# Graph product of the last stage in two row halves, router of the last stage laid out twice

## The chip, the cores and the metric

One program on one core of a Trainium2 chip. The metric is the device time of the whole program in microseconds (us), from the first to the last instruction with what the launch adds. Times of single instructions are read from one profiled execution.

## The reference, cut to what matters

The kernel computes two rounds of (graph layer, then mixture of experts) over 128 graphs of 64 nodes with 128 channels. The change touches only the second round:

```python
# adj: (128, 64, 64), regrouped; x: tokens x 128 channels
d = (sum(adj, -1) + 1e-5) ** -0.5
x = x + (d * adj * d) @ (layernorm(x) @ W) + b            # graph layer: a 64 x 64 matrix per graph
f = layernorm(x)
r = relu(f @ router_w1 + router_b1)                       # 128 -> 64
p = softmax(r @ router_w2 + router_b2); top-2 of 6 experts # 64 -> 6
x = x + sum over the two chosen experts of weight * mlp_e(f)   # 128 -> 128 -> 128 -> 128
```

A graph has 64 nodes, so two graphs fill the 128 rows (partitions) of a tile, and the product with `adj` mixes only rows of the same graph.

## The kernel before, in words

The program has three stages. The first (0 to 346 us of the profile) is the first round up to its router. The second ("blocks", 354 to 652 us) runs 136 blocks of 128 gathered rows through their expert, one block after the other. The third ("the sweep", from 653 us to the end) is the second round: 16 groups `g` of 512 tokens, each as `TG` = 4 tiles of 128 tokens (two graphs each).

In the sweep every engine runs its own list of steps for an iteration, and the lists of one iteration hold steps of several groups: PE (TensorE) works on `g[0]`, `g[1]` and `g[2]` at once. No scheduler is involved. The order on each engine is the order of the calls in its `body`, and semaphores tie the engines together. The steps of PE that matter, in their order: `aT` (graph product, L2175), `c(1)`, `gnn` (times the weight, L2186), `c(2)`, `gateT_`, then a long row of expert products, `f3T` (transposition of the normalised rows), `b(2)`, `b(3)`, `rh` (router layer 1, L2203), `b(4)`, `a(4)`, `logits` (router layer 2, L2212), `a(2)`, `b(5)`, `c(0)`, `a(1)`, `a(0)`, and the next `aT`. `a`, `b` and `c` are the three layers of the experts (L2245, L2269, L2277).

What waits for what around them:
- `aT` writes PSUM bank 2; ACT (ScalarE) copies it to `tT` (L1569), and only then can PE do `gnn`. Between them PE has `c(1)`.
- `logits` writes bank 7; DVE (VectorE) adds the bias (`lg_`, L1897), finds the largest (`top_`, L1905), does the gating product `m(2)` (L1892, tiles prod<-act,gate_bc), then `dtop_` (L1933) and `xn_`. ACT waits for `dtop` with `etop_` (L1591), and its next step is `ra(2)` (L1555), the evacuation of `a(2)`. PE's `a(0)` uses the bank of `a(2)` and waits for `ra(2)`.
- POOL (GpSimd) issues eight gathers in an iteration (L1481), and between them the elementwise `rs` (L1499) and `xb_` (L1491, 128x512, both operands in SBUF). The fifth gather stands just ahead of `xb_`.

The first group's graph product does not run in the sweep. `first_group` places it, one tile for each block, into the last blocks (L2114, L2116), in PSUM bank 0.

A float32 product is seen in the profile as two LDWEIGHTS and two MATMUL records, which I call its two pieces; `aT` and `logits` have four products and so eight pieces in each group. `PEld` is the loading of the stationary operand.

In `aT` the moving operand is `adjt[p][:, t, :]`, a 128 x 128 matrix with one graph in its upper left and one in its lower right quarter; the two other quarters are set to zero by POOL once (L1439), ahead of the load. `rhT` has 64 rows: `logits` uses the upper half of the array alone.

Of the kernel before, what the change touches and what calls it, by code (L numbers as in the profile page):

```python
# [20 lines left out]
P = 128  # L21
# [74 lines left out]
def build(nc, x, adj_t, gnn0_w, gnn0_b, ln1, ln2, wqkv, wo, router0, w13, w2, gnn1_w, gnn1_b,  # L96
# [14 lines left out]
    with ExitStack() as whole:  # L111
# [1089 lines left out]
        with ExitStack() as ctx:  # L1201
# [13 lines left out]
            gw, gb = sb("gw1", [P, C]), sb("gb1", [P, C])  # L1215
            rw1, rw1_hi, rw1_lo = sb("rw1", [P, RH]), sb("rw1_hi", [P, RH], f32r), sb("rw1_lo", [P, RH], f32r)
            rb1, rw2, rb2 = sb("rb1", [RH, 1]), sb("rw2", [RH, 8]), sb("rb2", [P, 8])
            ew1_hi, ew1_lo = sb("ew1_hi", [P, NE1 * C], f32r), sb("ew1_lo", [P, NE1 * C], f32r)
# [4 lines left out]

            adjt = [sb(f"adjt_c{i}", [P, TG, C]) for i in range(2)]
            rows = [sb(f"expert_rows{i}", [P, 2 * TG, C]) for i in range(2)]
# [17 lines left out]
            tabled, TABLE = sem("tabled"), 20  # L1243
            tile_aT, tile_tT, tile_gnn = sem("tile_aT"), sem("tile_tT"), sem("tile_gnn")
# [3 lines left out]
            rhT = sb("rhT", [RH, GT])  # L1248
            lg, top, topi = sb("lg_c", [P, TG, 8]), sb("top_c", [P, TG, 8]), sb("topi_c", [P, TG, 8], u32)
# [13 lines left out]
            gates_stored, stored = sem("gates_stored"), sem("stored")  # L1263
            NW = 14

            B_AT, B_GNN, B_F3T, B_RH, B_LOGITS, B_GATET = 2, 6, 5, 2, 7, 0
            B_A, B_B = (5, 7, 5, 3, 4, 7), (5, 0, 1, 6, 0, 3)
# [79 lines left out]
            with nc.Block() as block:  # L1347
                @block.sync
                def _(sp):
# [30 lines left out]
                    def lda(g, p):  # L1380
                        if g is not None:
                            if first(g):
                                sp.wait_ge(zeroed, 2)
                            if has(g - 2):
                                sp.wait_ge(at["aT"], g - 1)
                            src = adj_t[bass.ds(g * GT, GT), :].rearrange("(t b m) n -> b m t n", b=2, m=NN)
                            for k in range(2):
                                sp.dma_start(adjt[p][k * NN:(k + 1) * NN, :, k * NN:(k + 1) * NN], src[k]).then_inc(ld_adj[p], 16)

# [40 lines left out]
                def _(pool):  # L1430
                    def last_group():

                        G.memset(prod[:, :, HIDP:KC * P], 0.0).then_inc(padded, 1)
                        for n in range(2 * TG):
                            G.indirect_dma_start(
                                out=slots_in, out_offset=bass.IndirectOffsetOnAxis(ap=slot_now0[1][:, n:n + 1], axis=0),
                                in_=flat[1][:, n // 2, :], in_offset=None, bounds_check=ROWS - 1).then_inc(scattered[1], 16)
                            if n in (1, 3):
                                G.memset(adjt[n // 2][:, :, :], 0.0).then_inc(zeroed, 1)  # L1439
                            elif n == 5:  # L1440
                                G.memset(gate[:, :, :], 0.0).then_inc(zeroed, 1)

                    def weights():

                        G.memset(mhalf[:, :], -0.5).then_inc(padded, 1)
                        G.memset(rb2[:, :], -1e30).then_inc(zeroed, 1)
                        G.memset(eb3[:, :], 0.0).then_inc(zeroed, 1)
                        pool.wait_ge(padded, 2)
                        pool.wait_ge(zeroed, 5)
                        for dst, src in ((gw[:, :], gnn1_w), (gb[:, :], gnn1_b.partition_broadcast(P)), (rw1[:, :], r1_w1),  # L1450
                                         (rb1[:, :], r1_b1), (rw2[:, :], r1_w2), (rb2[:, 0:NE1], r1_b2.partition_broadcast(P)),
                                         (ew1[:, :], e_w1), (ew2[:, :], e_w2), (ew3[:, :], e_w3), (eb1[:, :], e_b1), (eb2[:, :], e_b2),
                                         (eb3[0:NE1, :], e_b3), (eb3[8:8 + NE1, :], e_b3), (eb3[16:16 + NE1, :], e_b3)):
# [73 lines left out]
                def _(act):  # L1527
# [36 lines left out]
                    def tT_(g):  # L1564
                        if g is not None:
                            act.wait_ge(at["aT"], g + 1)
                            if has(g - 1):
                                act.wait_ge(at["gnn"], g)
                            S.activation(tT[:, :, :], banks[B_AT][:, :], ACT.Copy).then_inc(at["tT"], 1)  # L1569

# [7 lines left out]
                    def rhr(g):  # L1578

                        if g is not None:  # L1580
                            act.wait_ge(at["rh"], g + 1)
                            if has(g - 1):
                                act.wait_ge(at["logits"], g)
                            S.activation(rhT[:, :], banks[B_RH][0:RH, :], ACT.Relu, bias=rb1[:, :]).then_inc(at["rhr"], 1)

# [58 lines left out]
                def _(dve):  # L1644
# [249 lines left out]
                    def lg_(g):  # L1894
                        if g is not None:
                            dve.wait_ge(at["logits"], g + 1)
                            V.tensor_tensor(lg[:, :, :], banks[B_LOGITS][:, 0:TG * 8].rearrange("p (t e) -> p t e", t=TG),  # L1897
                                            rb2[:, :].unsqueeze(1).broadcast_to([P, TG, 8]), ALU.add).then_inc(router.sem, 1)

# [197 lines left out]
                def _(pe):  # L2097
# [5 lines left out]
                    def first_group(t):  # L2103

                        if t == 0:
                            pe.wait_ge(prepared, 8)
                            pe.wait_ge(ld_adj[0], 32)
                            pe.wait_ge(at["xn"], 1)
# [58 lines left out]
                    def aT(g, p):  # L2167

                        if g is not None:
                            pe.wait_ge(ld_adj[p], pair(g, p) * 2)  # L2170
# [210 lines left out]
```

## Time and profile before

| | |
|---|---|
| time, median of 3 runs | 992.95 us (992.92 to 993.37) |
| span of the profiled execution | 991.6 us |
| PE busy | 930.0 us, 94% of the span |
| DVE / ACT / POOL busy | 73% / 58% / 46% |
| an iteration of the sweep | 20.2 to 21.2 us (start of `logits` to start of the next) |

The profile gives for each stretch what an engine did, and what ended the idle time ahead of an instruction. The profiled execution's span is 1.35 us shorter than the median of the runs, which holds what lies around the span as well. A MATMUL record starts when the instruction is taken up and can include waiting for its weights; so a distance between the starts of two neighbours says more than the length of one.

### The profile page before, as it was taken

Reading aid. Unit: us, or ns where it says so; the run is one execution under the profiler, and the core shown is the slowest. Engines: PE = TensorE matmul, PEld = TensorE weight load, DVE = VectorE, ACT = ScalarE, POOL = GpSimd, SP = SyncE. Lnnn points to the kernel's source line nnn. Section 1 sums busy time; section 2 is a strip of 40 time slices with the busy share of each in tenths; the row PEclk is TensorE's granted clock in tenths of the full one; section 3 lists DMA queues with packets and bytes.
Section 4 is the critical chain, followed back from the end, with each engine's and each line's share of the span. In section 5 each row is a group of like instructions: output and inputs, shape, how many; then the busy total and the mean of one; then the engine's idle time right before and its main releaser. Section 6 shows DMA issues by size and latency. Waiting matters only on the chain.

```text
span 991.6 us, 26476 instructions
## 1 busy us (share of the span) xinstructions
PE 930.0 (94%) x6766; PEld 735.8 (74%) x6767; DVE 721.4 (73%) x3070; ACT 573.6 (58%) x1498; POOL 459.7 (46%) x458
## 2 busy tenths in 40 slices
PE   5899999999999589999999999989999999999998
PEld 4777877787778479999999999965665556555564
DVE  4688888888887556455555546678888888888863
ACT  2587677767777434555555555445455554555554
POOL 2357777777777585002001000256665656656410
PEclk9999999999999889999999999999999999999999
DMA  5411111111110042222222222224333443334422
GB/s 180 134 36 47 44 53 48 43 45 50 48 45 26 35 137 61 64 61 73 67 66 70 62 60 71 68 61 152 112 107 105 137 146 113 106 104 126 149 81 85
DMA packets 88607, 81.32 MB, mean 82 GB/s; under 512 B 26894, under 2 KB 81568, under 8 KB 86256
## 3 DMA queue, kind: packets, MB, share of 16 engines
q1 hardware_dynamic: 78624, 62.21, 20.1%
q0 software_dynamic: 8784, 18.16, 5.8%
q10 hardware_dynamic: 1152, 0.39, 0.2%
q8 instruction: 20, 0.33, 0.1%
q14 instruction: 27, 0.22, 0.1%
HBM read 57.46 MB, written 23.27 MB: 81 GB/s over the span
## 4 chain that ended last, share of the span: by engine, by line
PE 54%; issue 5%; POOL 3%; DVE 2%; ACT 1%; DMA 1%; POOLq 0%; DVEq 0%; ACTq 0%
PE bank L2147 13%; PE bank L2130 10%; PE bank L2277 6%; PE bank L2269 6%; PE bank L2245 5%; PE bank L2155 4%; POOL expert_rows L1481 2%; PE bank L2139 2%; PE bank L2186 1%; PE bank L2212 1%; PE bank L2175 1%; PE bank L2203 1%; ACT h L1555 1%; PE bank L2195 1%; PE bank L2291 1%
## 5 line engine op out<-in xcount | busy, mean ns | idle before, releaser
L1481 POOL DMA_INDIRECT expert_rows<-slots_out,slot_c x128 | 139.5, 1090 | 106.1 <-DVE ys L1728 75.3
L1720 DVE TENSOR_TENSOR prod<-bank,act 128x342 f32<-128x342 f32 x136 | 70.0, 515 | 102.8 <-ACT act L1538 102.6
L362 POOL DMA_INDIRECT slots_in<-flat,slot_now x120 | 120.5, 1004 | 37.7 <-issue 37.5
L2130 PE MATMUL bank<-w_sb,prodT 128*128 x816 | 118.9, 282 | 0.9 <-ACT prodT L1543 0.7
L1538 ACT ACTIVATE act<-bank 128x342 f32<-128x342 f32 x136 | 62.0, 456 | 96.0 <-PE bank L2147 96.0
L2130 PEld LDWEIGHTS bank<-w_sb,prodT 128*128 128x128 f32 x816 | 101.7, 191 | 8.5 <-issue 6.0
L2147 PE MATMUL bank<-w_hi,xT_hi 128*128 x272 | 99.0, 364 | 0.1
L2269 PE MATMUL bank<-h,ew 128*128 128x512 f32 x192 | 97.6, 606 | 0.0
L2147 PE MATMUL bank<-w_hi,xT_lo 128*128 x272 | 87.0, 320 | 0.0
L2147 PE MATMUL bank<-w_lo,xT_hi 128*128 x272 | 86.6, 319 | 0.0
L1555 ACT ACTIVATE h<-bank,eb 128x512 f32<-128x512 f32 x96 | 63.6, 680 | 14.1 <-PE bank L2245 13.8
L1499 POOL TENSOR_TENSOR rs_c<-var_c,mhalf 128x4 f32<-128x4 f32 x16 | 20.2, 1261 | 109.4 <-DVE var_c L1816 109.4
L2245 PE MATMUL bank<-f_hi,ew_hi 128*128 128x512 f32 x96 | 66.3, 691 | 3.9 <-ACT h L1555 3.9
L1548 ACT ACTIVATE xT_hi<-bank 128x128 fp32r<-128x128 f32 x136 | 37.7, 277 | 52.3 <-PE bank L2139 52.3
L2155 PE MATMUL bank<-cst,prod 128*128 128x128 f32 x408 | 66.8, 273 | 0.1
L1543 ACT ACTIVATE prodT<-bank 128x384 f32<-128x384 f32 x136 | 66.1, 486 | 0.9 <-PE bank L2155 0.8
L452 ACT ACTIVATE pr<-sc,nmx 128x64 f32<-128x64 f32 x256 | 62.7, 337 | 1.3 <-DVE nmx L680 1.3
L1562 ACT ACTIVATE flat<-bank,eb 128x512 f32<-128x512 f32 x64 | 43.5, 681 | 26.7 <-DVE ys L1892 17.4
L1506 POOL TENSOR_TENSOR rs_d<-var_d,mhalf 128x4 f32<-128x4 f32 x16 | 17.2, 1076 | 84.3 <-DVE var_d L1864 84.3
L2155 PEld LDWEIGHTS bank<-cst,prod 128*128 128x128 f32 x408 | 52.7, 140 | 3.0 <-DVE prod L1720 0.5
L2147 PEld LDWEIGHTS bank<-w_hi,xT_hi 128*128 128x128 f32 x272 | 51.4, 189 | 2.0 <-issue 1.2
L2147 PEld LDWEIGHTS bank<-w_lo,xT_hi 128*128 128x128 f32 x272 | 52.0, 191 | 0.0
(320 smaller groups left out, 2481.6 us busy)
## 6 DMA issues: line engine op xcount, KB each, us to landing
gate_bc<-gates_dram SPq DMA_DIRECT2D x16, 1536.0 KB
xs<-slots_in SPq DMA_DIRECT2D x136, 64.0 KB, 1.8
slots_out<-ys SPq DMA_DIRECT2D x68, 128.0 KB, 1.8
base_all<-in_x SPq DMA_DIRECT2D x16, 256.0 KB, 2.8
out<-ob SPq DMA_DIRECT2D x16, 256.0 KB, 2.7
w_lo<-in_w SPq DMA_DIRECT2D x1, 2736.0 KB, 9.9
adjt<-in_adj_t SPq DMA_DIRECT2D x32, 64.0 KB, 2.3
slots_in<-flat,slot_now POOLq DMA_INDIRECT x128
```

What stands on the lines that cost most here:

```text
L362: G.indirect_dma_start(out=slots_in, out_offset=bass.IndirectOffsetOnAxis(ap=slot_now0[p][:, n:n + 1], axis=0), in_=flat[p][:, n // 2, :], ...
L452: last = S.activation(pr[:, t, h, :], sc[:, t, h, :], ACT.Exp, scale=SCALE, bias=nmx[:, t * NH + h:t * NH + h + 1])
L1481: G.indirect_dma_start(out=rows[p][:, n, :], out_offset=None, in_=slots_out[0:filled(g) * P, :], in_offset=bass.IndirectOffsetOnAxis(ap=sl ...
L1538: S.activation(act1[:, u % 2, :], banks[1 + u % 2][:, 0:HIDP], ACT.Silu).then_inc(silu_done, 1)
L1543: S.activation(prodT[:, (u - 3) % 2, :], banks[5 + (u - 3) % 2][:, 0:KC * P], ACT.Copy).then_inc(prodT_copied, 1)
L1555: S.activation(h1[n % 3][:, :], banks[B_A[n]][:, :], ACT.Relu, bias=eb1[:, n:n + 1]).then_inc(per["ra"].sem, 1)
L1720: V.tensor_tensor(prod[:, u % 2, 0:HIDP], banks[3 + u % 2][:, 0:HIDP], act1[:, u % 2, :], ALU.mult).then_inc(prod_done, 1)
L2130: last = T.matmul(banks[7][:, 0:C], prodT[:, u % 2, n * P:(n + 1) * P], w2_sb[:, bass.ds(e * (KC * C) + n * C, C)], start=n == 0, stop=n = ...
L2147: last = T.matmul(banks[1 + 2 * n + par][:, 0:HIDP], xx[:, par, :], ww[:, bass.ds(e * (2 * HIDP) + n * HIDP, HIDP)], start=q == 0, stop=q ...
L2155: last = T.transpose(banks[5 + u % 2][:, n * P:(n + 1) * P], prod[:, u % 2, n * P:(n + 1) * P], ident)
L2245: last = T.matmul(banks[B_A[n]][:, :], ww[:, w], ff[p][:, :], start=q == 0, stop=q == 2)
L2269: T.matmul(banks[B_B[n]][:, :], ew2[:, n * C:(n + 1) * C], h1[n % 3][:, :], start=True, stop=True).then_inc(per["b"].sem, 1)
```

## The change

1. `adjt` holds only the 64 columns that are not zero. It is loaded by one DMA for a group instead of two, and is no longer cleared by POOL.
2. `aT` does for each tile two products: rows 0 to 63 (first graph) into bank 2, rows 64 to 127 (second graph) into bank 0, with 64 columns each. ACT copies the two banks to `tT` with two instructions of 128x4x64 instead of one of 128x512.
3. `first_group` does the same with both halves in bank 0, with a wait for the first half ahead of the second.
4. `router_w1`, its bias and `router_w2` are loaded twice, so that `rh` gives each of the 64 outputs twice, in rows 0 to 63 and 64 to 127. `logits` takes the upper rows for tiles 0 and 2 (bank 7) and the lower ones for tiles 1 and 3 (bank 2). DVE adds the bias in two instructions.
5. `aT` waits for `lg` of the group before (it waited for `rhr`) and for `rb4` of the one before that.

```diff
-                            src = adj_t[bass.ds(g * GT, GT), :].rearrange("(t b m) n -> b m t n", b=2, m=NN)
-                            for k in range(2):
-                                sp.dma_start(adjt[p][k * NN:(k + 1) * NN, :, k * NN:(k + 1) * NN], src[k]).then_inc(ld_adj[p], 16)
+                            sp.dma_start(adjt[p][:, :, :], adj_t[bass.ds(g * GT, GT), :].rearrange("(t p) n -> p t n", p=P)).then_inc(ld_adj[p], 16)
...
-                            if n in (1, 3):
-                                G.memset(adjt[n // 2][:, :, :], 0.0).then_inc(zeroed, 1)
...
-                            S.activation(tT[:, :, :], banks[B_AT][:, :], ACT.Copy).then_inc(at["tT"], 1)
+                            for b in range(2):
+                                last = S.activation(tT[:, :, b * NN:(b + 1) * NN], banks[B_AT[b]][:, 0:TG * NN].rearrange("p (t n) -> p t n", t=TG), ACT.Copy)
+                            last.then_inc(at["tT"], 1)
...
-                            V.tensor_tensor(lg[:, :, :], banks[B_LOGITS][:, 0:TG * 8].rearrange("p (t e) -> p t e", t=TG),
-                                            rb2[:, :].unsqueeze(1).broadcast_to([P, TG, 8]), ALU.add).then_inc(router.sem, 1)
+                            for j in range(2):
+                                last = V.tensor_tensor(lg[:, j:TG:2, :], banks[B_LOGITS[j]][:, 0:TG * 4].rearrange("p (t e) -> p t e", t=TG // 2),
+                                                       rb2[:, :].unsqueeze(1).broadcast_to([P, TG // 2, 8]), ALU.add)
+                            last.then_inc(router.sem, 1)
...
-                            T.matmul(banks[0][:, P:2 * P], xn[:, t, :], adjt[0][:, t, :], start=True, stop=True).then_inc(tile_aT if t < TG - 1 else at["aT"], 1)
+                            T.matmul(banks[0][:, P:P + NN], xn[0:NN, t, :], adjt[0][0:NN, t, :], start=True, stop=True).then_inc(tile_half, 1)
+                            pe.wait_ge(tile_half, t + 1)
+                            T.matmul(banks[0][:, P + NN:2 * P], xn[NN:P, t, :], adjt[0][NN:P, t, :], start=True, stop=True).then_inc(tile_aT if t < TG - 1 else at["aT"], 1)
...
                             if exists(g - 1):
-                                pe.wait_ge(at["rhr"], g)
-                            for t in range(TG):
-                                last = T.matmul(banks[B_AT][:, t * P:(t + 1) * P], xn[:, t, :], adjt[p][:, t, :], start=True, stop=True)
+                                pe.wait_ge(router.sem, router.at("lg", g - 1))
+                            if exists(g - 2):
+                                pe.wait_ge(per["rb"].sem, per["rb"].at("rb4", g - 2))
+                            for t in range(TG):
+                                for b in range(2):
+                                    last = T.matmul(banks[B_AT[b]][:, t * NN:(t + 1) * NN], xn[b * NN:(b + 1) * NN, t, :],
+                                                    adjt[p][b * NN:(b + 1) * NN, t, :], start=True, stop=True)
...
-                                last = T.matmul(banks[B_RH][0:RH, :], ww[:, :], ff[p][:, :], start=q == 0, stop=q == 2)
+                                last = T.matmul(banks[B_RH][:, :], ww[:, :], ff[p][:, :], start=q == 0, stop=q == 2)
...
-                                last = T.matmul(banks[B_LOGITS][:, t * 8:t * 8 + 8], rhT[:, t * P:(t + 1) * P], rw2[:, :], start=True, stop=True)
+                                half = slice(t % 2 * RH, (t % 2 + 1) * RH)
+                                last = T.matmul(banks[B_LOGITS[t % 2]][:, t // 2 * 8:t // 2 * 8 + 8], rhT[half, t * P:(t + 1) * P], rw2[half, :], start=True, stop=True)
```

On PE, in an iteration of the sweep, from the last product of `a(0)` to `c(2)`, before (the shape is that of the output):

```order
L2245 MATMUL bank<-f_hi,ew_lo 128x512
L2175 MATMUL bank<-adjt_c,xn_c 128x128 x4
L2277 MATMUL bank<-ys,ew 128x512
L2186 MATMUL bank<-gw,tT_c 128x128 x4
L2277 MATMUL bank<-prod,ew 128x512
```

and in the changed kernel:

```order
L2250 MATMUL bank<-f_hi,ew_lo 128x512
L2178 MATMUL bank<-adjt_c,xn_c 128x64 x8
L2282 MATMUL bank<-ys,ew 128x512
L2190 MATMUL bank<-gw,tT_c 128x128 x4
L2282 MATMUL bank<-prod,ew 128x512
```

The place of every step is the same; four products of 128 columns have become eight of 64. On PE in the last blocks, at the first group's first tile, as a difference:

```order
 L2130 ISA
 L2130 MATMUL bank<-w_sb,prodT 128x128
-L2114 MATMUL bank<-adjt_c,xn_c 128x128
+L2112 MATMUL bank<-adjt_c,xn_c 128x64
+L2114 MATMUL bank<-adjt_c,xn_c 128x64
 L2139 MATMUL bank<-cst,xs 128x128
```

Here too only the product is split, between the same neighbours; L2112 and L2114 are the two halves with the wait between them. On no other engine does a step change its place.

## Rows read from the trace of the kernel before

**Rows 1.** The page, part 1: busy us (share of the span) xinstructions of each engine.

```profile
PE 930.0 (94%) x6766; PEld 735.8 (74%) x6767; DVE 721.4 (73%) x3070; ACT 573.6 (58%) x1498; POOL 459.7 (46%) x458
```

**Rows 2.** Timeline of PE, 711.5 to 725.2: start, us, engine, line, what, [idle before].

```profile
715.39 0.40 PE L2245 MATMUL bank<-f_hi,ew_lo 128*128 128x512 f32 x1
715.72 1.05 PE L2212 MATMUL bank<-rw,rhT 64*128 64x8 f32 x8
716.71 0.51 PE L2245 MATMUL bank<-f_hi,ew_hi 128*128 128x512 f32 x1
717.05 0.40 PE L2245 MATMUL bank<-f_lo,ew_hi 128*128 128x512 f32 x1
...
720.26 0.50 PE L2245 MATMUL bank<-f_hi,ew_hi 128*128 128x512 f32 x1 [0.17 <-ACT h L1555]
...
720.83 0.39 PE L2245 MATMUL bank<-f_hi,ew_lo 128*128 128x512 f32 x1
721.05 1.05 PE L2175 MATMUL bank<-adjt_c,xn_c 128*128 128x128 f32 x8
721.95 1.02 PE L2277 MATMUL bank<-ys,ew 128*128 128x512 f32 x2
722.81 1.15 PE L2186 MATMUL bank<-gw,tT_c 128*128 128x128 f32 x8
```

**Rows 3.** Timeline of PE, 943.5 to 949.8, the same steps twelve groups later.

```profile
943.65 1.05 PE L2212 MATMUL bank<-rw,rhT 64*128 64x8 f32 x8
...
948.56 1.05 PE L2175 MATMUL bank<-adjt_c,xn_c 128*128 128x128 f32 x8
```

**Rows 4.** Timeline of PE's weight loads, 715.3 to 724.2.

```profile
722.79 0.97 PEld L2186 LDWEIGHTS bank<-gw,tT_c 128*128 128x128 f32 x8 [0.65 <-ACT tT_c L1569]
```

**Rows 5.** Timeline of DVE, 716.7 to 720.4.

```profile
716.82 0.19 DVE L1897 TENSOR_TENSOR lg_c<-bank,rb 128x32 f32<-128x32 f32 x1 [0.43 <-PE bank L2212]
...
717.33 1.93 DVE L1892 TENSOR_TENSOR prod<-act,gate_bc 128x512 f32<-128x512 f32 x1
719.19 0.18 DVE L1933 TENSOR_TENSOR dtop_c<-top_c 128x32 f32<-128x32 f32 x1
```

**Rows 6.** Timeline of POOL, 712.8 to 720.6.

```profile
716.31 1.08 POOL L1481 DMA_INDIRECT expert_rows<-slots_out,slot_c  x1 [0.20 <-issue]
717.42 1.28 POOL L1491 TENSOR_TENSOR xb_c<-x,gb 128x512 f32<-128x512 f32 x1
```

**Rows 7.** Timeline of ACT, 719.3 to 723.3.

```profile
719.40 0.23 ACT L1591 ACTIVATE etop_c<-dtop_c 128x32 f32<-128x32 f32 x1 [2.81 <-DVE dtop_c L1933]
719.54 0.67 ACT L1555 ACTIVATE h<-bank,eb 128x512 f32<-128x512 f32 x1
...
722.15 0.60 ACT L1569 ACTIVATE tT_c<-bank 128x512 f32<-128x512 f32 x1 [0.81 <-PE bank L2175]
```

**Rows 8.** L1892 from 690 to 940: duration ns min/median/max.

```profile
L1892 DVE TENSOR_TENSOR prod<-act,gate_bc x24: 673/680/2210, 696.7 to 933.8; 128x512 f32<-128x512 f32 x24
```

**Rows 9.** Timeline of PE, 85.2 to 87.5, first stage.

```profile
85.81 1.09 PE L1030 MATMUL bank<-k_rot,q_rot 32*64 32x64 f32 x64
```

**Rows 10.** Timeline of ACT, 25.8 to 28, first stage: copies of 256 columns.

```profile
26.12 0.38 ACT L440 ACTIVATE v_diag<-bank 64x256 f32<-64x256 f32 x1 [3.08 <-PE bank L1015]
26.51 0.38 ACT L441 ACTIVATE v_diag<-bank 64x256 f32<-64x256 f32 x1
```

**Rows 11.** Timeline of PE, 628.1 to 631.6: first group in the blocks.

```profile
631.07 0.39 PE L2114 MATMUL bank<-adjt_c,xn_c 128*128 128x128 f32 x2
631.29 0.39 PE L2116 MATMUL bank<-gw,tT_c 128*128 128x128 f32 x2
```

**Rows 12.** Timeline of DVE, 659 to 662.4.

```profile
659.79 2.03 DVE L1919 CAST topf_c<-topi_c 128x8 f32<-128x8 uint32 x1
```

**Rows 13.** Timeline of POOL, 659.0 to 662.4.

```profile
659.48 1.01 POOL L1481 DMA_INDIRECT expert_rows<-slots_out,slot_c  x1 [0.30 <-issue]
660.51 1.27 POOL L1491 TENSOR_TENSOR xb_c<-x,gb 128x512 f32<-128x512 f32 x1
```

More of the change, by code:

```diff
@@ L1215, in build @@
             gw, gb = sb("gw1", [P, C]), sb("gb1", [P, C])
-            rw1, rw1_hi, rw1_lo = sb("rw1", [P, RH]), sb("rw1_hi", [P, RH], f32r), sb("rw1_lo", [P, RH], f32r)
-            rb1, rw2, rb2 = sb("rb1", [RH, 1]), sb("rw2", [RH, 8]), sb("rb2", [P, 8])
+            rw1, rw1_hi, rw1_lo = sb("rw1", [P, P]), sb("rw1_hi", [P, P], f32r), sb("rw1_lo", [P, P], f32r)
+            rb1, rw2, rb2 = sb("rb1", [P, 1]), sb("rw2", [P, 8]), sb("rb2", [P, 8])
             ew1_hi, ew1_lo = sb("ew1_hi", [P, NE1 * C], f32r), sb("ew1_lo", [P, NE1 * C], f32r)
@@ L1222, in build @@
             mhalf = sb("mhalf1", [P, NG * TG])
-            adjt = [sb(f"adjt_c{i}", [P, TG, C]) for i in range(2)]
+            adjt = [sb(f"adjt_c{i}", [P, TG, NN]) for i in range(2)]
             rows = [sb(f"expert_rows{i}", [P, 2 * TG, C]) for i in range(2)]
@@ L1243, in build @@
             tabled, TABLE = sem("tabled"), 20
-            tile_aT, tile_tT, tile_gnn = sem("tile_aT"), sem("tile_tT"), sem("tile_gnn")
+            tile_half, tile_aT, tile_tT, tile_gnn = sem("tile_half"), sem("tile_aT"), sem("tile_tT"), sem("tile_gnn")
             AHEAD = LOOPED + 8
@@ L1247, in build @@
             st_b, mv_b, var_b, rs_b = sb("st_d", [P, TG, 6]), sb("mv_d", [P, TG, 2]), sb("var_d", [P, TG]), sb("rs_d", [P, TG])
-            rhT = sb("rhT", [RH, GT])
+            rhT = sb("rhT", [P, GT])
             lg, top, topi = sb("lg_c", [P, TG, 8]), sb("top_c", [P, TG, 8]), sb("topi_c", [P, TG, 8], u32)
@@ L1263, in build @@
             gates_stored, stored = sem("gates_stored"), sem("stored")
-            NW = 14
-            B_AT, B_GNN, B_F3T, B_RH, B_LOGITS, B_GATET = 2, 6, 5, 2, 7, 0
+            NW = 17
+            B_AT, B_GNN, B_F3T, B_RH, B_LOGITS, B_GATET = (2, 0), 6, 5, 2, (7, 2), 0
             B_A, B_B = (5, 7, 5, 3, 4, 7), (5, 0, 1, 6, 0, 3)
@@ L1381, in lda @@
                         if g is not None:
-                            if first(g):
-                                sp.wait_ge(zeroed, 2)
                             if has(g - 2):
                                 sp.wait_ge(at["aT"], g - 1)
-                            src = adj_t[bass.ds(g * GT, GT), :].rearrange("(t b m) n -> b m t n", b=2, m=NN)
-                            for k in range(2):
-                                sp.dma_start(adjt[p][k * NN:(k + 1) * NN, :, k * NN:(k + 1) * NN], src[k]).then_inc(ld_adj[p], 16)
+                            sp.dma_start(adjt[p][:, :, :], adj_t[bass.ds(g * GT, GT), :].rearrange("(t p) n -> p t n", p=P)).then_inc(ld_adj[p], 16)
                     def gst(g, p):
@@ L1437, in last_group @@
                                 in_=flat[1][:, n // 2, :], in_offset=None, bounds_check=ROWS - 1).then_inc(scattered[1], 16)
-                            if n in (1, 3):
-                                G.memset(adjt[n // 2][:, :, :], 0.0).then_inc(zeroed, 1)
-                            elif n == 5:
+                            if n == 5:
                                 G.memset(gate[:, :, :], 0.0).then_inc(zeroed, 1)
@@ L1448, in weights @@
                         pool.wait_ge(padded, 2)
-                        pool.wait_ge(zeroed, 5)
-                        for dst, src in ((gw[:, :], gnn1_w), (gb[:, :], gnn1_b.partition_broadcast(P)), (rw1[:, :], r1_w1),
-                                         (rb1[:, :], r1_b1), (rw2[:, :], r1_w2), (rb2[:, 0:NE1], r1_b2.partition_broadcast(P)),
+                        pool.wait_ge(zeroed, 3)
+                        for dst, src in ((gw[:, :], gnn1_w), (gb[:, :], gnn1_b.partition_broadcast(P)), (rw1[:, 0:RH], r1_w1), (rw1[:, RH:P], r1_w1),
+                                         (rb1[0:RH, :], r1_b1), (rb1[RH:P, :], r1_b1), (rw2[0:RH, :], r1_w2), (rw2[RH:P, :], r1_w2), (rb2[:, 0:NE1], r1_b2.partition_broadcast(P)),
                                          (ew1[:, :], e_w1), (ew2[:, :], e_w2), (ew3[:, :], e_w3), (eb1[:, :], e_b1), (eb2[:, :], e_b2),
@@ L1583, in rhr @@
                                 act.wait_ge(at["logits"], g)
-                            S.activation(rhT[:, :], banks[B_RH][0:RH, :], ACT.Relu, bias=rb1[:, :]).then_inc(at["rhr"], 1)
+                            S.activation(rhT[:, :], banks[B_RH][:, :], ACT.Relu, bias=rb1[:, :]).then_inc(at["rhr"], 1)
                     def etop_(g):
@@ L2106, in first_group @@
                             pe.wait_ge(prepared, 8)
-                            pe.wait_ge(ld_adj[0], 32)
+                            pe.wait_ge(ld_adj[0], 16)
                             pe.wait_ge(at["xn"], 1)
@@ L2169, in aT @@
                         if g is not None:
-                            pe.wait_ge(ld_adj[p], pair(g, p) * 2)
+                            pe.wait_ge(ld_adj[p], pair(g, p))
                             pe.wait_ge(at["xn"], g + 1)
                             if exists(g - 1):
-                                pe.wait_ge(at["rhr"], g)
+                                pe.wait_ge(router.sem, router.at("lg", g - 1))
+                            if exists(g - 2):
+                                pe.wait_ge(per["rb"].sem, per["rb"].at("rb4", g - 2))
                             for t in range(TG):
-                                last = T.matmul(banks[B_AT][:, t * P:(t + 1) * P], xn[:, t, :], adjt[p][:, t, :], start=True, stop=True)
+                                for b in range(2):
+                                    last = T.matmul(banks[B_AT[b]][:, t * NN:(t + 1) * NN], xn[b * NN:(b + 1) * NN, t, :],
+                                                    adjt[p][b * NN:(b + 1) * NN, t, :], start=True, stop=True)
                             last.then_inc(at["aT"], 1)
```

## The prediction

> **What bounds the kernel now.** I read the page's busy shares first: PE works for 94% of the span, the next engine for 73% [rows 1]. So what a step costs PE is what counts, if no chain of waits stands behind it. I then read PE's timeline through one iteration of the sweep (the 715 to 725 us stretch) and looked for places where PE is not simply handing over from one product to the next.
>
> There are two. The first is `a(0)` at 720.26, which waits for `ra(2)` on ACT [rows 2]. How long PE stands there is best seen from the distance of the starts of `logits` and `aT`: 721.05 - 715.72 = 5.33 us here [rows 2], and 948.56 - 943.65 = 4.91 us for the same steps in a group where `a(0)` waits for nothing [rows 3]. So 0.42 us are lost here. In the 14 groups that have both steps I measured distances of 4.90 to 5.92 us in this way; over 4.9 they lose 7.0 us in all.
> The chain behind it: `logits` ends, DVE adds the bias at 716.82, and starts `m(2)` at 717.33. That product takes 1.93 us, though its median is 0.68 [rows 5, 8]. It is held by POOL: `xb_` runs from 717.42 to 718.70 [rows 6], `m(2)` ends 0.56 us later at 719.26, and only then come `dtop` [rows 5], `etop` at 719.40 and `ra(2)`, 719.54 to 720.21 [rows 7], and `a(0)`. In 11 of the 12 groups between 690 and 927 us `m(2)` takes 1.62 to 2.21 us, and each time it ends 0.56 us after `xb_`, whether it started 0.23 us after it or 0.37 us ahead of it. (In the twelfth DVE is held by `xb_` one step earlier.) So in these groups the time of `a(0)` is set by POOL's `xb_`, not by `logits`. POOL's steps hang on `var0` and, ahead of that, on DVE's `lo` of the iteration, not on `logits`.
>
> The second place is `gnn`. Its weights can be loaded only when `tT` is there: the load starts at 722.79, 0.04 after the copy's end at 722.75 (722.15 + 0.60) [rows 4, 7]. With a load of about 0.11 the first piece really starts near 722.90, while `c(1)` ended at 722.81 [rows 2]. `c(1)` covers the copy of `tT` just short of fully.
>
> **The change part by part.** The pace of float32 pieces: `logits` moves only 8 columns and `aT` 128, and yet eight pieces of either last 1.05 us [rows 2], 0.11 us apart. So the load of 128 stationary columns sets the pace, and halving the moving columns in `aT` brings nothing by itself. What can bring something is that the row halves run side by side. The first stage shows it: 64 pieces of a 32-row form, spread over the four row groups, last 1.09 us together [rows 9], 0.013 us a piece after taking off one piece's length. So I take two halves to run side by side, each at 0.11.
>
> A second cost goes with that: changing between 128-row and 64-row products. `logits` has it today. A full-height product is followed by the next start after 0.22 us (720.83 to 721.05), but `logits` starts 0.33 after (715.39 to 715.72), and the second product of `a(2)` starts 0.34 after the first where 0.23 is the rule [rows 2]. From 715.39 + 0.22 = 715.61 to 717.05 - 0.23 = 716.82 `logits` takes 1.21 us of PE; eight pieces are 0.90, so the two changes of height cost 0.31. `aT` takes 0.90 (721.05 to 721.95) and has no change of height [rows 2].
>
> - `logits` (16 times): four pieces for each half, 0.45, and the changes, 0.31: 0.77 for 1.21, 0.44 less.
> - `aT` (15 times): eight pieces for each half, 0.90, and now changes of height, 0.31, and 0.05 for the longer last piece: 1.25, 0.35 more.
> - `tT`: `aT` ends 0.17 later (0.22 for the change on the way in, 0.05 less for the shorter last piece), so the copy starts at 722.32. Two copies of 256 columns: 0.38 each and at the most 0.39 apart [rows 10]; at the least 0.28, if they overlap by 0.1. The end is 722.98 to 723.09 for 722.75. `gnn`'s first piece is then ready at 723.13 to 723.24, while `c(1)`, shifted by 0.35, ends at 723.16. Before it was 722.90: 0.26 to 0.34 more for the pair `aT` and `gnn`. I take 0.27, as `c(1)` now hides the copy. The first of the 15 pairs costs nothing: there `gateT_` waits anyway for a DVE cast that `xb_` holds up [rows 12, 13]. 14 x 0.27 = 3.8 us.
> - `first_group` (4 times, inside the blocks, where PE hands over without a gap: L2114 at 631.07, L2116 at 631.29, 0.22 us for the two pieces [rows 11]). Now four pieces, 0.44, the changes of height, 0.31, and the wait for the own first half: a piece's length of about 0.22, 0.05 for the semaphore and a load of 0.11, less the 0.11 already counted: 0.27. In all 1.02 for 0.22, 0.8 more; PE is what the blocks wait for, so 4 x 0.8 = 3.2 us. Lower bound 0.22 a tile (two more pieces and nothing else), 0.9 us.
> - What of the gain of `logits` arrives: where `xb_` holds `m(2)`, nothing. DVE reaches `m(2)` 0.38 us earlier (0.44 less 0.06 for the second bias instruction) and waits 0.38 longer; `a(0)` starts when it did. The two last groups have no `xb_` in the way: 2 x 0.44 = 0.9 us less.
> - `rh` with 128 outputs instead of 64: the load is longer but lies under products of 512 columns; its three products keep their pace. The bias copy has the same columns. The DMA in one piece, the wait for `lg` (DVE does it ahead of `xn`, for which `aT` waits anyway) and the wait for `rb4` of two groups back: nothing. Fewer clearings and three more small loads on POOL at 350 to 365 us: between 1 us less and 1 us more; I take 0.
>
> Sum: 991.6 + 3.8 + 3.2 - 0.9 = 997.7 us for the span, and with the 1.35 us between span and median 999.0 us.
>
> **The rivals.**
> 1. *`m(2)` gets ahead of `xb_`* (faster). At 716.95 `m(2)` would start 0.47 us ahead of the recorded start of `xb_`. If it then runs freely, each of the 11 groups gains the 0.44 of `logits` and its stall at `a(0)` (5.1 us over the 11): 9.9 us less, 989.1 us. It decides at the moment from which POOL holds DVE. Against it: `m(2)` was held in a group where it started 0.37 us ahead, and at 659.79 a cast that started 0.31 after the gather and 0.72 ahead of `xb_` was held until `xb_` ended [rows 12, 13]. After the change `m(2)` starts 0.64 after its gather (716.31) [rows 6]. For it: POOL's recorded starts need not be the moment of holding, and the cast is another kind of instruction. The Trainium skill (SBUF — State Buffer, "SBUF: two separate sides") says that of a DVE instruction with two SBUF inputs and a GpSimd one that reads SBUF, whichever starts first has the port pair for its whole length, and the other blocks fully. By that rule this rival would be the forecast, 989; the full blocking agrees with the trace, but the recorded order does not: `m(2)` starts at 717.33, `xb_` at 717.42, and `m(2)` is the one held. Chance 0.17, and 0.08 more that it holds in about half of the groups, near 993.
> 2. *The halves do not run side by side* (much slower). Then `aT` takes 16 x 0.11, 0.9 more each, and `logits` gains nothing: 14 x 0.9 + 0.9 = 13.5 more, 1012.5 us. Against it speaks the first stage's form [rows 9], which however has 32 rows and 64 columns. Chance 0.08.
> 3. *`aT` gains what its name promises* (the split does not act as I think: no change of height is paid, and pieces of 64 columns go at 0.055): `aT` 0.45 less instead of 0.35 more. 14 x 0.45 = 6.3 less in place of 3.8 more: 988.9 us. The Trainium skill (TensorEngine Tiling (Array Packing), "Theoretical Speedup") puts a small dimension of 64 at up to twice the speed. The sum by that is this rival's. The pace of `logits` with its 8 columns [rows 2] speaks against it. Chance 0.05.
>
> **How the numbers follow.** The forecast, POOL still holding `m(2)` and the changes of height paid, gets 0.62. Its own range is 995.5 (first group at its lower bound, `tT` well hidden, 1 us won on POOL) to 1002.5 (`tT` at 0.34, one more piece of 0.11 in each `aT`, 1 us lost on POOL). For 8 in 10 the range reaches down over rivals 1 and 3 and leaves rival 2 out: 988.5 to 1003.5. What a measurement can tell from no change is about 0.2%, 991.0 to 994.9. Faster: 0.17 + 0.05 = 0.22. Same: the half way of rival 1 and a little of the forecast's lower edge, 0.10. Slower: 0.60 + 0.08 = 0.68.
>
> **What would show it.** In the changed kernel's timeline of PE `logits` should last about 0.6 us instead of 1.05, and `c(1)` start 1.2 to 1.3 us after `aT`. The distance from the start of `logits` to that of `aT` stays at 5.0 to 5.6 us in the middle groups, with longer idle time ahead of `a(0)`; `m(2)` still takes 1.6 to 2.6 us and ends 0.56 after `xb_`. The two tT copies take 0.66 to 0.77 together. The blocks 128 to 131 are 0.8 us longer each. I am wrong if `m(2)` shrinks to 0.68 in most groups (rival 1), if `logits` still lasts 1.05 (rival 2), or if `aT` and `c(1)` are under 0.9 apart (rival 3); and in the size, if PE finds other work to hide the first group's waits.

## The result and the profile after

The changed kernel takes 1023.52 us (median of 4 runs, 1022.57 to 1025.32), the kernel before beside it 993.16 us (992.92 to 993.52): ratio 1.0309, 95% interval 1.0295 to 1.0324. That is 30.4 us slower; the prediction had 6.0 of them. The direction was right, the size was not: 1023.5 lies outside the range of 988.5 to 1003.5.

Where the time is, I looked for by stages. This is the view of stretches of the changed kernel (first round, blocks, last stage; after the lengths come each engine's busy time and count, the granted TensorE clock, the DMA share and GB/s):

```profile
0.00:346.00 346.00, 298.18 (x3248) 252.91 (x3249) 276.71 (x1302) 237.55 (x769) 226.07 (x228) 0.99 0.18 59
346.00:653.00 307.00, 301.47 (x2203) 285.88 (x2204) 170.05 (x507) 151.73 (x406) 54.75 (x60) 0.99 0.25 71
653.00:1023.50 370.50, 336.52 (x1445) 196.22 (x1443) 275.19 (x1279) 185.62 (x338) 182.82 (x171) 0.96 0.33 106
```

The last stage is 31.9 us longer by this cut (the same cut of the kernel before gives 338.6 us with a clock of 0.99). The last blocks take up 4.6 us of that, since the first `logits` start at 660.15 instead of 655.54. PE's work has grown by only 9 us, and its clock is lower. So PE stands somewhere. Its timeline in an ordinary iteration shows nothing of the kind; one at the end of a pass of the loop does:

```profile
776.59 1.12 PE L2274 MATMUL bank<-h,ew 128*128 128x512 f32 x2
777.55 0.60 PE L2296 MATMUL bank<-cst,prodT 128*128 128x128 f32 x4
782.74 1.11 PE L2199 MATMUL bank<-cst,f 128*128 128x128 f32 x4 [4.58 <-DVE f L1868]
783.64 3.62 PE L2274 MATMUL bank<-h,ew 128*128 128x512 f32 x4
786.28 1.42 PE L2207 MATMUL bank<-f_hi,rw_hi 128*128 128x512 f32 x1
```

`f3T` waits 4.58 us for `f3` on DVE. A wait of 4.5 to 4.7 us comes four times, at 782.7, 831.6, 880.0 and 927.9 us, in every second group, and never in the first groups. This is DVE ahead of it:

```profile
773.21 0.18 DVE L1852 BATCH_NORM_AGGREGATE mv_d<-st_d 128x2 f32<-128x6 f32 x1
773.30 0.28 DVE L1852 BATCH_NORM_AGGREGATE mv_d<-st_d 128x2 f32<-128x6 f32 x3
775.90 0.17 DVE L1771 COPY slot_c<-slots_all 128x8 uint32 x1 [2.32 <-issue]
779.39 0.17 DVE L1772 COPY gate_c<-gates_all 128x8 f32 x1 [3.32 <-issue]
779.59 0.17 DVE L1860 TENSOR_SCALAR var_d<-mv_d 128x4 f32<-128x4 f32 x1
779.85 1.14 DVE L1779 SCALAR_TENSOR_TENSOR x2a<-expert_rows,gate_c,base_all 128x128 f32<-128x128 f32 x4
781.27 1.34 DVE L1868 TENSOR_SCALAR f<-base_all,mv_d,rs_d 128x128 f32 x4 [0.27 <-POOL rs_d L1500]
```

Two tiny copies, the first two vector instructions of the loop's body, come 2.32 and 3.32 us late, and "issue" says that they waited for nothing the profile shows. `rs_d` on POOL and `f3` hang on them. The third place is the list of DMA queues, here over one pass of the loop (800.0 to 848.4 us), with the queue's kind, packets, MB and share:

```profile
q1 hardware_dynamic: 2424, 3.96, 24.5%
q0 software_dynamic: 512, 1.05, 8.0%
q14 instruction: 6, 0.05, 0.4%
```

The queue that loads instructions moves six packets of 8 KB in this pass, at 800.2, 808.2, 821.4, 822.6, 826.4 and 831.0 us; five come again in each of the next passes, the one at 808.2 does not. The same stretch of the kernel before has no row of that queue at all; over the whole run its count is 27, in the changed kernel 47.

A third part of the cost follows from the wait. PE stands idle from 778.2 us. At 781.9 us the granted clock falls to the lower of its two levels (1.2 GHz) and stays there until 788.7. The same fall comes at 829.7, 877.4 and 928.6 us, in or just behind such a wait:

```profile
755.00:777.50 22.50, 21.79 (x95) 12.41 (x94) 15.92 (x74) 11.99 (x22) 11.03 (x10) 1.00 0.37 118
777.50:782.70 5.20, 0.66 (x5) 0.42 (x4) 2.92 (x12) 0.69 (x1) 2.49 (x3) 0.92 0.62 244
782.70:789.00 6.30, 6.26 (x14) 3.64 (x14) 5.03 (x19) 2.85 (x5) 5.24 (x5) 0.52 0.39 104
789.00:800.00 11.00, 11.00 (x61) 7.05 (x60) 7.74 (x45) 5.23 (x12) 5.10 (x5) 1.00 0.10 25
```

From `f3T` to `a(4)` PE takes 6.24 us there (782.74 to 788.98) for 3.31 in the iteration before (757.00 to 760.31). So a pass loses 4.6 us in the wait and 2.9 in the slow stretch after it, and gets some back where PE would have waited for `h`: a pass lasts 48.1 to 48.7 us instead of 41.2 to 41.9 (start of `logits` to the start two groups later).

### The profile page after: what moved, and what is told of

It reads as the page before. It is cut to its first block, busy times and chain, and to the rows that moved or that the text cites. A ratio compares the mean times of both kernels' runs of the same rounds, so it can differ in the third digit from the quotient of the medians.

```text
span 1023.5 us, 26737 instructions
## 1 busy us (share of the span) xinstructions
PE 936.2 (91%) x6894; PEld 735.0 (72%) x6895; DVE 722.0 (71%) x3086; ACT 574.9 (56%) x1513; POOL 463.6 (45%) x459
## 4 chain that ended last, share of the span: by engine, by line
PE 35%; issue 16%; POOL 11%; DVE 2%; ACT 1%; DMA 1%; POOLq 0%; DVEq 0%; ACTq 0%
PE bank L2147 12%; PE bank L2130 10%; POOL expert_rows L1475 8%; PE bank L2155 4%; PE bank L2282 2%; PE bank L2139 1%; POOL rs_c L1493 1%; PE bank L2250 1%; PE bank L2274 1%; POOL xb_c L1485 1%; PE bank L2165 1%; PE bank L2178 1%; PE bank L2190 1%; DMA slots_out<-ys 1%; DVE base_all L1836 0%
## 5 line engine op out<-in xcount | busy, mean ns | idle before, releaser
L2274 PE MATMUL bank<-h,ew 128*128 128x512 f32 x192 | 103.5, 639 | 0.0
L2274 PEld LDWEIGHTS bank<-h,ew 128*128 128x128 f32 x192 | 36.0, 201 | 24.3 <-issue 21.2
```

The lines of the kernel that those rows point to most:

```text
L2274: T.matmul(banks[B_B[n]][:, :], ew2[:, n * C:(n + 1) * C], h1[n % 3][:, :], start=True, stop=True).then_inc(per["b"].sem, 1)
```

## The theories

**A, place of the code.** `sweep` is a hardware loop of two groups a pass; its body on DVE is 263 instructions before, 265 after (255 and 257 in the program, and 8 index searches that are two instructions each). The second bias instruction of `lg` adds one in each of four unrolled groups ahead of the loop, and two in the body. The loop makes five passes; the first is entered from ahead and has no stall. Instructions come in packets of 8 KB. If a piece is 128 instructions and the body fits three pieces, nothing is reloaded; if it touches a fourth, each pass reloads them. The two late copies stand on either side of such a boundary.

**B, the added work**, or a wait of it, slows DVE at that place. **C, traffic**: the gate broadcast, whose transfer falls into the same microseconds (DMA share 0.62 above), holds up DVE's start.

## The experiments

The runs are numbered as in their labels: run 1 is e1, and so on.

**1 to 3. Dummy instructions.** Memsets of a tile of its own, in blocks where DVE is half idle, put the loop at another place and do nothing else.

```
 ahead(k)
+for n in range(8):            # 4, 12 and 2 in the others
+    if k == LOOPED + 7 + n % 4:
+        V.memset(pad[:, n:n + 1], 0.0)
```

> The changed kernel with eight dummy VectorE memsets (of a tile of their own, 60 ns each, in blocks 127 to 130 where VectorE is half idle) ahead of the hardware loop of the last stage; nothing else differs. Theory A, placement: the changed kernel put four more VectorE instructions ahead of the loop and two into it, so that the loop (some 265 instructions) now begins 3 or 4 before a boundary of 128 instructions (8 KB) and reaches into a fourth such piece; each pass of two groups then reloads instructions and VectorE stands 2.3 and 3.3 us at the two copies at the loop's head. Eight more move the head past the boundary: both stalls and the 8 KB instruction transfers inside the loop go, the four passes fall from 48.2 to 41 to 42 us, and the time from 1023.5 to about 996 (993 to 999). Rival B, the added work itself (a second logit read, two copies of the aT product, row halves) or its waits slow VectorE at that place: the stalls stay, 1022 to 1025. Rival C, the gate broadcast's DMA traffic delays VectorE there: stays as well.

Measured: 998.61 us, ratio 1.0062 (1.0043 to 1.0082). The changed kernel with eight more instructions is 25 us faster. Its queue of instructions over the pass from 794.7 to 836.5 us:

```profile
q14 instruction: 1, 0.01, 0.0%
```

> The kernel before with four of the same dummy memsets in the same place, the change itself left out altogether. Theory A: the loop's head moves to the place at which it stands in the changed kernel, and its 263 instructions reach a fourth piece of 128; stalls of some 2.3 and 3.3 us at the two copies in four passes, five or six 8 KB transfers of instructions a pass, 1016 to 1023 against 993. Rivals B and C: nothing of the change is in it, so 993 to 994.

Measured: 1022.52 us, ratio 1.0293 (1.0268 to 1.0318). Four dummy memsets do to the kernel before what the change seemed to do: the same two copies are late.

```profile
873.15 0.17 DVE L1777 COPY slot_c<-slots_all 128x8 uint32 x1 [2.28 <-issue]
876.49 0.17 DVE L1778 COPY gate_c<-gates_all 128x8 f32 x1 [3.17 <-issue]
```

> The kernel before with twelve dummy memsets, three times as much added work as in the run with four. Theory A: the head now lies behind the boundary, the loop fits three pieces again: 993 to 994.5, no stalls. If added VectorE work, not its place, were what costs, it would be slower than the run with four.

Measured: 993.6 us, ratio 1.0008 (0.9992 to 1.0024). Three times the dummy work costs nothing. Theory A holds. B falls with the first run (the work is still there, the stalls are gone) and the second (no part of the change, stalls). C falls with the second too.

**4 and 9. The edge.**

> The kernel before with two dummy memsets: locates the edge. By the count of instructions the loop before ends 0 or 1 instruction ahead of the boundary, so two more should bring its last one or two instructions (the branch among them) into a fourth piece. Theory A: stalls as with four, 1014 to 1023; if the edge lies further, or if only the place between the two copies matters, 993 to 994.

Measured: 1028.26 us, ratio 1.0362 (1.0335 to 1.0390). The second stall has moved two instructions on in the body, so it has stayed where it was in the stream:

```profile
822.50 0.17 DVE L1777 COPY slot_c<-slots_all 128x8 uint32 x1 [3.42 <-issue]
822.62 0.17 DVE L1778 COPY gate_c<-gates_all 128x8 f32 x1
827.14 0.17 DVE L1866 TENSOR_SCALAR var_d<-mv_d 128x4 f32<-128x4 f32 x1 [4.35 <-issue]
```

> The kernel before with one dummy memset. With two, and with four, the second stall stood at the same absolute place of the instruction stream (before the third, and before the second, vector instruction of the loop), which puts the boundary at the loop's fifth or sixth instruction of the run with two. Counted from there the loop before ends on the last or the last but one place of its third piece. So one more instruction either still fits (993 to 994) or already stalls (1019 to 1029), nothing in between.

Measured: ratio 1.0024 (0.9994 to 1.0054), no instruction transfer between 860 and 900 us. (This run and runs 10 to 12 were on a chip with a lower granted clock, where the kernel before takes 1051.65 us; each ratio is to runs on the same chip.) So one more instruction fits and a second does not: the kernel before had exactly one instruction to spare.

How large a piece is needs a second look. By the two places of the second stall (a register instruction stands between the copies, two ahead of `var_d`) the boundary is behind the loop's fifth or sixth instruction of the run with two. With the sixth, 263 - 6 = 257 are left, and with one dummy 256. That fits a boundary every 128 instructions with three pieces allowed, but also one every 256 with two allowed, so the places alone don't decide. The packets do. In the changed kernel one pass has them at 822.6 (the jump back to the loop's head), 826.4, 831.0, 848.6 and 869.7 us. DVE goes through 126 instructions from 826.4 to 848.6, 128 from there to 869.7, and 127 from 751.6 to 772.5 in the first pass. So a piece is 128 instructions, and each is asked for about one piece ahead of its use. The second stall is then the case in which it can't be: only a few instructions lie between the head and the boundary, and the packet for what follows starts at 826.4, after the late copy at 824.8.

The Trainium skill (Runtime: NRT & Kernel Launch, "Instruction fetch mechanics") states that a taken branch whose target isn't in the current window of two pages forces a load before execution can go on; the runs agree that a jump back can force one. Its size of a page, 16 KiB, differs from the 8 KB that q14 moves here (q8 does move 16 KB: 21 packets, 0.34 MB). It gives most engines 32 KiB for instructions. At the 64 bytes each that follow from it, a loop of 263 is by estimate about half of that, so its length alone would leave room. By the packets a pass that touches four pieces loads five, the fifth lying behind the loop's end, and by the same estimate that is 40 KiB, while three and the one behind them are 32. This fits the runs; how much the engine holds was not tested otherwise.

With the place of the loop out of the way, the rest is the prediction's own subject. All further kernels have the loop clear of the boundary.

**5 to 7. The parts alone.**

> The router's part of the change alone (first layer twice side by side, logit products on alternate row halves into two banks, two reads of them); the graph product and the first group stay as before; eight dummy memsets keep VectorE's loop clear of the boundary. The step of the prediction under test: the logit products start-to-next fall from 0.99 to 0.54 us, but the TensorE wait for the hidden layer h behind them grows by the same 0.45, since the multiply m(2) on VectorE ends 0.56 us after GpSimd's xb_ whatever TensorE does; gain only where that wait is absent (the last two groups): 0 to 1.5 us faster than before, ratio 0.9985 to 1.000. Rival: the logit gain is free in each of 16 groups, 7 us faster, ratio 0.993.

```
-last = T.matmul(banks[B_LOGITS][:, t * 8:t * 8 + 8], rhT[:, t * P:(t + 1) * P], rw2[:, :], ...)
+half = slice(t % 2 * RH, (t % 2 + 1) * RH)
+last = T.matmul(banks[B_LOGITS[t % 2]][:, t // 2 * 8:t // 2 * 8 + 8], rhT[half, t * P:(t + 1) * P], rw2[half, :], ...)
```

Measured: 993.11 us, ratio 1.0008 (0.9992 to 1.0023). Nothing of the 7 us arrives. In the whole last stage PE waits 8.0 us ahead of the `a` products, for 3.9 in the kernel before:

```profile
L2253 PE MATMUL bank<-f_hi,ew_hi 128*128 128x512 f32 x96 | 65.7, 684 | 8.0 <-ACT h L1557 8.0
L1894 DVE TENSOR_TENSOR prod<-act,gate_bc 128x512 f32<-128x512 f32 x32 | 39.5, 1233 | 0.0
```

(After the count: us busy, ns of one, and the idle time before them with what ended it.)

> The graph product of groups 1 to 15 in two row halves from the compact adjacency, with its two banks, its added wait and the two copies; router as before, first group's product whole (from a zero-padded tile of its own); padded with twelve memsets so that VectorE's loop head lies where it does in the others. By the prediction +0.27 us a group, +3.8 over 14; by the trace of the padded changed kernel (product to next 0.89 to 1.04, to the node product 0.88 to 0.96, that one 0.99 to 0.90) +0.16 a group, +2.4. Ratio 1.002 to 1.004. Rival: the halves do run side by side and pay elsewhere, ratio 0.999 to 1.001.

```
-last = T.matmul(banks[B_AT][:, t * P:(t + 1) * P], xn[:, t, :], adjt[p][:, t, :], ...)
+for b in range(2):
+    last = T.matmul(banks[B_AT[b]][:, t * NN:(t + 1) * NN], xn[b * NN:(b + 1) * NN, t, :], adjt[p][b * NN:(b + 1) * NN, t, :], ...)
```

Measured: 996.08 us, ratio 1.0032 (1.0022 to 1.0042), 3.2 us, for 1.0008 (0.9992 to 1.0024) of the twelve memsets alone (run 3): the split product is a loss by itself.

> The changed kernel with the eight memsets, the first group's product (blocks 128 to 131) left whole as before, from a zero-padded tile. The prediction put 0.8 us on each of these four blocks; the padded changed kernel shows 3.06 to 3.33 us for blocks that took 2.28 to 2.51. Expected 3.3 us below the padded changed kernel, ratio to before 1.002 to 1.004 in place of 1.0062. Rival: other work fills the gap by then (the stage after waits for something else at its start), ratio still 1.005 to 1.007.

```
-T.matmul(banks[0][:, P:P + NN], xn[0:NN, t, :], adjt[0][0:NN, t, :], ...).then_inc(tile_half, 1)
-pe.wait_ge(tile_half, t + 1)
-T.matmul(banks[0][:, P + NN:2 * P], xn[NN:P, t, :], adjt[0][NN:P, t, :], ...).then_inc(...)
+T.matmul(banks[0][:, P:2 * P], xn[:, t, :], adjw[:, t, :], ...).then_inc(...)
```

Measured: 995.99 us, ratio 1.0033 (1.0018 to 1.0048) for the 1.0062 of the first run: the difference of 0.29%, 2.9 us, sits in the four blocks. The two intervals touch, but the trace says the same: those blocks are back at 2.3 to 2.5 us.

**8, 10 to 12. Is it really `xb_` that holds `m(2)`?** One line moved on POOL:

```
+xb_(g[1])
 gt(4, g[0], p[0])
-xb_(g[1])
 gt(5, g[0], p[0])
```

> The router-only kernel with one GpSimd instruction moved: xb_ (1.28 us) stands before the fifth gather of its round in place of behind it, so it starts some 1.1 us earlier, and the multiply m(2) that it held up ends earlier. If that hold is what turned the logit gain into a wait: the distance from the logit products to the graph product loses 0.4 to 0.8 us in 14 groups, 6 to 11 us faster than before, ratio 0.989 to 0.994. Rival: xb_ only holds up other VectorE work (the small router steps ahead of m(2)) and m(2) ends as late, or h is late for another reason: within 1.5 us of the router-only kernel.

Measured: 985.52 us, ratio 0.9933 (0.9916 to 0.9949), 7.3 us below the kernel before. This beats both kernels. The same two rows:

```profile
L2253 PE MATMUL bank<-f_hi,ew_hi 128*128 128x512 f32 x96 | 65.7, 685 | 2.2 <-ACT h L1557 2.0
L1894 DVE TENSOR_TENSOR prod<-act,gate_bc 128x512 f32<-128x512 f32 x32 | 21.6, 676 | 0.0
```

The multiply is at its free 0.68 us on average, PE's wait for `h` is down from 8.0 to 2.0. POOL and DVE of one group:

```profile
794.39 1.27 POOL L1493 TENSOR_TENSOR xb_c<-x,gb 128x512 f32<-128x512 f32 x1
794.53 1.16 DVE L1824 COPY deg<-deg_all 128x4 f32 x1 [0.44 <-POOL rs_c L1501]
796.25 0.67 DVE L1894 TENSOR_TENSOR prod<-act,gate_bc 128x512 f32<-128x512 f32 x1
```

Somebody is still held, a copy of four columns for 1.16 us, but it stands ahead of the logits' bias, for which there is more time.

> The kernel before with xb_ one place earlier on GpSimd and nothing of the change. Its TensorE waits 3.9 us in all for the hidden layer h in the last stage, against 8.0 with the router's part and 2.2 with that part and the earlier xb_. If the hold of m(2) by xb_ is the cause, most of these 3.9 us go: 989 to 991, ratio 0.996 to 0.998, less than with the router's part (0.9933). Rival: the earlier xb_ is itself the gain in the run before, whatever the logits do: ratio 0.993.

Measured: ratio 1.0024 (0.9988 to 1.0061): neither. The distance from `logits` to `aT` did fall, to a mean of 4.91 us over the third to fourteenth group (5.39 in run 9 on the same chip), and PE hardly waits for `h` any more (0.3 us in all); but `gnn` now comes later, 1.51 us behind the start of `c(1)` on average over the same groups for 0.89. That gave the gain of 0.48 back.

> The whole change (with its split graph product and first group), eight memsets, and xb_ one place earlier. The padded whole change was at 1.0062; the earlier xb_ took 0.75% from the router-only kernel. If the parts add up: 0.998 to 1.0005, so the split graph product and first group, 0.6% in all, use up what the router's part gives. Rival: the longer copies of the graph product on ScalarE hold up h in place of m(2): 1.002 to 1.006.

Measured: ratio 1.0306 (1.0255 to 1.0358), slower by far, and not for the loop's place (14 `slot_c` copies, none late; 27 instruction packets). The trace shows the same thing as in the run before, only larger, in 13 groups:

```profile
872.65 1.11 PE L2183 MATMUL bank<-adjt_c,xn_c 64*128 64x64 f32 x16
873.69 1.12 PE L2287 MATMUL bank<-ys,ew 128*128 128x512 f32 x2
875.38 0.66 ACT L1566 ACTIVATE tT_c<-bank 128x256 f32<-128x256 f32 x2 [2.42 <-remote]
876.10 1.16 PE L2195 MATMUL bank<-gw,tT_c 128*128 128x128 f32 x8 [1.28 <-ACT tT_c L1566]
```

The graph product ends by its records near 873.8, but its semaphore rises at 875.36 and the copy starts at 875.38. From the start of the last graph piece to that of the copy it is 0.31 or 0.32 us in the other kernels (but for the first group of runs 8 and 12), 0.6 to 1.3 in most groups of run 10, and 1.5 to 2.07 here. Both expectations miss this. It accounts for only part of the 3%: in the profiled execution (1093.57 us, the longest of the six) the stretch from the first `logits` to the end is 353.4 us, for 336.8 in run 9. The other half of what that execution has over run 9 lies ahead of the sweep, where the kernels differ in little but the first group's product, and is not explained.

> The router-only kernel with xb_ one place later (behind the sixth gather) in place of earlier: it starts some 1.3 us later than m(2) does, so m(2) should run against a gather alone. If only an overlap with xb_ lengthens m(2): m(2) 0.7 to 1.2 us, and a gain like that of the earlier xb_ (0.991 to 0.995) unless xb_ now holds up the scaling xn_ behind it, on which the graph product waits: 0.996 to 1.001. If gathers lengthen m(2) as well: 1.8 us or more, and no gain.

Measured: ratio 0.9959 (0.9924 to 0.9993), between the two cases:

```profile
852.38 1.08 POOL L1483 DMA_INDIRECT expert_rows<-slots_out,slot_c  x1 [0.20 <-issue]
854.81 1.30 POOL L1493 TENSOR_TENSOR xb_c<-x,gb 128x512 f32<-128x512 f32 x1
853.07 0.67 DVE L1894 TENSOR_TENSOR prod<-act,gate_bc 128x512 f32<-128x512 f32 x1
853.76 2.70 DVE L1833 TENSOR_SCALAR xn_c<-x,mv_c,xscale 128x128 f32<-128x128 f32 x4
```

`m(2)` runs freely beside a gather, so gathers don't hold it; `xb_` now holds the scaling `xn`, 2.70 us for 1.10, and PE waits ahead of the graph product, though by little (at most 1.2 us in the five groups from 800 to 900 us).

## Why the prediction was right and wrong

**The step that failed** is the term "0.06 for the second bias instruction". It costs about that where it stands (two take 0.24 us for one of 0.17 to 0.19), and 25 us because it is there (1023.5 against 998.6 with the loop moved off the boundary). I had costed instructions by duration alone; the number of instructions in and ahead of a loop was no term of the sum, and no rival had it. The profile before showed that no instructions were loaded between 800 and 848 us; it did not show that the loop ended one instruction ahead of a boundary. A count of the loop's body gives only its length; the place of the boundary I know from the runs with dummies.

**The rest of the sum holds in total, in part by luck.** With the loop clear of the boundary the change is 1.0062 times before, 6.2 us; the forecast was +6.0. The terms are less exact than that: `aT` and `gnn` cost 1.8 us less than forecast, the last two groups gave 0.4 less, the middle groups cost 0.6 more, and the blocks began later by 1.1, which is noise. By its terms, from the padded changed kernel:

```profile
803.75 0.62 PE L2222 MATMUL bank<-rw,rhT 64*128 64x8 f32 x8
804.29 0.50 PE L2255 MATMUL bank<-f_hi,ew_hi 128*128 128x512 f32 x1
808.50 0.50 PE L2255 MATMUL bank<-f_hi,ew_hi 128*128 128x512 f32 x1 [0.83 <-ACT h L1551]
809.40 1.11 PE L2183 MATMUL bank<-adjt_c,xn_c 64*128 64x64 f32 x16
810.43 1.13 PE L2287 MATMUL bank<-ys,ew 128*128 128x512 f32 x2
```

- *`logits` 0.44 less.* From its start to the next product's 0.54 us, before 0.99 (715.72 to 716.71) [rows 2]: 0.45 less. Right, and rival 2 (the halves don't run side by side) is out.
- *Nothing of it arrives in the middle groups.* From the next product to `aT` it takes 4.91 us (mean of the third to fourteenth group) for 4.42: 0.49 more for the 0.44 gained, so a group is 0.05 longer. With the router's part alone it is 4.81, 0.39 more. Right within 0.05; runs 5 and 8 show that it is `xb_` that does it. In one group: `xb_` ends at 806.83, `m(2)` takes 2.26 us and ends at 807.39, 0.56 later, as it did [rows 5, 6].
- *Rival 1* (`m(2)` gets ahead of `xb_`) did not happen by itself: in the padded kernel `m(2)` starts at 805.13, 0.42 us ahead of the recorded start of `xb_` at 805.55, and is held (starts on POOL are rough). The Trainium skill (SBUF — State Buffer, "SBUF: two separate sides") would let the first to start run to its end; by the records it is the first that is held, as before. The rival's price, about 10 us with its stalls, was of the right order: run 8, where `m(2)` runs freely in every group, gains 7.3.
- *`aT` and `gnn` 0.27 a group, 3.8 in all.* Measured 0.15 for `aT` (0.89 to 1.04), 0.08 ahead of `gnn` (0.88 to 0.96), and 0.08 back behind it (0.99 to 0.90): 0.15 a group on average (0.12 to 0.16), 2.0 us over the 14 groups. Mis-sized by 0.12 a group: for `aT` I had 0.35 more, with 0.31 for the change of height, and it took 0.15 more. Rival 3 (`aT` gains twofold) is out; for the up to twice the speed that it took from the Trainium skill (TensorEngine Tiling (Array Packing), "Theoretical Speedup") the split product costs 3.2 us alone (run 6).
- *The two last groups 0.9 less.* Only one of them gave it. From the last `logits` to the end it is 27.34 us for 27.79, 0.45 less. In the group before it `logits` to `aT` is 4.87 us for 4.90. The prediction saw no `xb_` in the way there. It isn't in the way of `m(2)`, which takes 0.67; but `xb_` (943.98 to 945.25 in the kernel before) holds the copy `deg`, which stands ahead of the bias of the logits. First the kernel before, then the padded one:

```profile
944.04 1.24 DVE L1822 COPY deg<-deg_all 128x4 f32<-128x4 f32 x1 [0.30 <-POOL rs_c L1499]
951.26 1.25 DVE L1820 COPY deg<-deg_all 128x4 f32<-128x4 f32 x1 [0.30 <-POOL rs_c L1495]
```

- *First group 0.8 a block.* The copy of `prodT` in each block of the padded kernel comes 3.06, 3.33, 3.33 and 3.33 us after the last for 2.28, 2.50, 2.51 and 2.51: 3.25 us for a predicted 3.2.
- *Start of the blocks, between -1 and +1.* The first block's copy of `prodT` starts 1.1 us later in the padded kernel (359.71 for 358.61), but also 0.9 later in run 3, 1.8 later in run 5 and 0.5 earlier in run 2, which leave this part alone or touch little of it: noise of that size.

## What to carry to other kernels

- A hardware loop of some 260 instructions has a place as well as a length. Before a change that adds even one instruction in or ahead of a loop is judged, read the instruction queue over one pass: none before and several after are the sign here that the place was measured, not the change. Two kernels are compared fairly only with the loop clear of a boundary in both; a few dummy instructions ahead of it settled it here in one run.
- A saving ahead of an instruction that another engine holds becomes a longer wait. Move what holds first (here one POOL line, 7.3 us together with the saving), then save.

## What had not been expected

- Two to four instructions of 60 ns cost a 992 us kernel 30 to 36 us. In a pass they bring stalls of 2.2 to 5.4 us each at two places of DVE, one at the jump back and one at the next boundary, and through PE's idle time a stretch of about 6 us at the lower clock.
- In these traces `xb_` on POOL holds whatever DVE instruction meets its start, down to a copy of four columns (1.16 to 1.24 us for 0.17), while in run 12 `m(2)` ran freely beside a gather of the same engine.
- An earlier `xb_` made the graph product's copy late by 0.3 to 1.8 us in two kernels and not in a third, with no wait in the trace that explains it; the signal from the graph product itself comes late. Two of them ran on the chip with the lower clock and the third on another; run 12, on the former, does not show it. Whether it is the place of some transfer, of the gathers or of the chip stays open.
